# Query tiles 1 to 3 prepared inside the attention slots, with a new order of loads, wide weight loads and three result transfers

## What is computed

```python
def _qdq(x):
    s = jnp.maximum(jnp.max(jnp.abs(x), axis=-1, keepdims=True) / 127.0, 1e-08)
    return jnp.clip(jnp.round(x / s), -127.0, 127.0) * s

# x: (8, 56, 256), ctx: (8, 1500, 256), 16 heads of 16
q = _qdq(_layernorm(x)) @ _qdq(wq).T + bq
k, v = jnp.split(ctx @ wkv.T + bkv, 2, axis=-1)
attn = jax.nn.softmax(jnp.einsum('bnhd,bmhd->bhnm', q, k) * scale, axis=-1)
o = jnp.einsum('bhnm,bmhd->bnhd', attn, v).reshape(B, N, C)
x = x + jnp.tanh(g_xattn[0]) * (_qdq(o) @ _qdq(wp).T + bp)
x = x + jnp.tanh(g_ffn[0]) * experts(_layernorm(x))
```

## Time and profile before

| what | us |
|---|---|
| time, median of 3 runs (lowest, highest) | 400.9 (397.43, 401.9) |
| time of the profiled execution | 397.17 |
| its span, first to last instruction | 395.4 |
| first matmul | 11.33 |
| first scores, slot 0 | 32.71 |
| scores of slot 5 | 60.30 |
| scores of slot 56 | 272.69 |

### The profile page before, as it was taken

How to read it: one execution, slowest core, us unless ns; L and a number is a source line. 1 busy time by engine, 2 the same in 40 slices (tenths; PEclk the granted TensorE clock), 3 DMA queues, 4 the chain that set the end, 5 groups by cost and what they waited for, 6 DMA issues and landing times.

```text
span 395.4 us, 14055 instructions
## 1 busy us (share of the span) xinstructions
PE 351.7 (89%) x5828; PEld 262.6 (66%) x5828; DVE 302.6 (77%) x652; ACT 251.1 (63%) x413; POOL 105.8 (27%) x99
## 2 busy tenths in 40 slices
PE   0896859999998998999899999899986779999994
PEld 0672538677766865867686686677664557888883
DVE  3988885776676677568568667676988998999994
ACT  3575737687676776767667676657672355667671
POOL 6152643023132322302233230001010104544541
PEclk9999989999999999999999999999999999999998
DMA  7979995284187256329417313664200008654101
GB/s 250 208 173 194 214 186 115 67 173 122 54 143 196 58 91 160 99 82 159 147 56 117 91 33 70 126 156 149 76 3 3 0 2 282 181 159 125 51 2 46
DMA packets 34561, 45.67 MB, mean 115 GB/s; under 512 B 4043, under 2 KB 30347, under 8 KB 34371
## 3 DMA queue, kind: packets, MB, share of 16 engines
q1 hardware_dynamic: 33443, 43.74, 47.0%
q0 software_dynamic: 640, 0.78, 1.1%
q10 hardware_dynamic: 416, 0.26, 0.3%
HBM read 25.08 MB, written 0.47 MB: 65 GB/s over the span
## 4 chain that ended last, share of the span: by engine, by line
PE 76%; DVE 14%; issue 5%; ACT 2%; POOL 2%; DMA 1%; DVEq 0%; ACTq 0%; POOLq 0%
PE PS L1055 38%; PE PS L1121 10%; PE PS L1098 9%; PE PS L1132 8%; PE PS L1404 3%; PE PS L1363 3%; PE PS L1108 2%; DVE mx L809 2%; DVE mtop L813 2%; PE PS L1387 1%; DMA x_in<-x 1%; DVE st L712 1%; DVE KN L758 1%; DVE cT L730 1%; POOL cT L399 1%
## 5 line engine op out<-in xcount | busy, mean ns | idle before, releaser
L809 DVE TENSOR_REDUCE mx<-PS 112x1 f32<-112x500 f32 (+1 forms) x128 | 114.2, 933 | 53.9 <-PE PS L1098 53.8
L1055 PE MATMUL PS<-cT,wkvT 128*128 128x500 f16 x288 | 71.1, 384 | 21.9 <-POOL slot_of L408 11.3
L507 ACT ACTIVATE PT_all<-PS 128x1344 f32<-128x1344 f32 x64 | 82.5, 1289 | 12.3 <-PE PS L1121 9.6
L1055 PE MATMUL PS<-wkvT,cT 128*125 128x256 f16 x576 | 71.9, 275 | 0.0
L1055 PEld LDWEIGHTS PS<-wkvT,cT 128*125 128x125 f16 x576 | 63.9, 137 | 5.3 <-issue 0.5
L1055 PEld LDWEIGHTS PS<-cT,wkvT 128*128 128x128 f16 x288 | 27.4, 99 | 54.0 <-POOL rank L407 11.3
L399 POOL TENSOR_TENSOR cT<-c_in,cT 128x1000 f16<-128x1000 f32 x18 | 37.4, 2082 | 90.5 <-ACT cT L485 90.5
L492 ACT ACTIVATE KN<-PS,col_in 128x500 f16<-128x500 f32 x48 | 32.5, 677 | 41.1 <-PE PS L1055 41.1
L1098 PE MATMUL PS<-arena,QC 96*112 96x500 f16 x192 | 51.7, 376 | 3.5 <-issue 3.3
L1121 PE MATMUL PS<-QC,arena 98*128 98x112 f16 x768 | 48.6, 213 | 3.0 <-ACT QC L527 2.9
L499 ACT ACTIVATE V<-PS 125x512 f32<-125x512 f32 x48 | 28.7, 598 | 30.0 <-PE PS L1055 30.0
(11 more groups left out here) (211 smaller groups left out, 435.2 us busy)
## 6 DMA issues: line engine op xcount, KB each, us to landing
arena<-KN SPq DMA_DIRECT2D x144, 125.0 KB, 3.6
c_in<-ctx SPq DMA_DIRECT2D x24, 500.0 KB, 5.0
cT<-W SPq DMA_DIRECT2D x11, 352.0 KB
c_in<-W SPq DMA_DIRECT2D x6, 352.0 KB
cT<-W SPq DMA_DIRECT2D x11, 176.0 KB
arena<-place_far SPq DMA_DIRECT2D x1, 1568.0 KB, 10.2
c_in<-W SPq DMA_DIRECT2D x6, 176.0 KB
PT_all<-L_xattn_wkv SPq DMA_DIRECT2D x1, 512.0 KB, 6.1
```

The lines of the kernel that those rows point to most:

```text
L507: act.activation(PT_all[:, u % 4, :].rearrange("p (c k) -> p c k", c=CH), PS[:, 3:6, 0:4 * TP], ACT.Exp, scale=SCORE).then_inc(s["exp_done ...
L809: dve.tensor_reduce(mx[:, u % 2, k:k + 1], PS[0:TP, k:1 + k * (CH - 1), 0:CW], AX.XY, ALU.max).then_inc(s["red_done"], 1)
L1055: ins = mm(out_, w(a, h), x_(b, h), start=first and k == 0, stop=last and k == len(todo) - 1)
```

## The change

The edits, with the names of the diff:

- **Late tiles.** Only token tile 0 is prepared ahead of the slots. Tile t = 1, 2, 3 is prepared in slots 16(t-1)+1 to 16(t-1)+10, one step in each: `tile_step` on DVE (normalise, maximum, scale, round, spread), `tile_to_turn` and `tile_product` on PE in bank 7, `tile_turned`, `tile_scaled`, `tile_high` on ACT. The low half of a tile is written by DVE at the end of slot 16(t-1)+10. `qn` is a buffer of its own.
- **Stacking.** SP issues the 6 transfers of a tile (`stack_queries`), behind the stacking of the first half of the keys of batch 2t. `queries` of batch n waits for both tiles' halves by `q_stacked0` and `q_stacked1`. POOL issues none. The wait of the exponential is gone.
- **Loads.** The key half of the weights and chunk 0 of the context come first, then the tokens, the value half, the query weights, chunks 1 and 2. The rows and the gate weights move from ACT's queue to SP's. Chunk 2 of batch 1 is asked for behind the stacking of K2 and the queries. DVE begins with the weights and chunk 0, and takes the query weights before tile 0.
- **Blocks.** K5 of batch 0 moves into slot 0 as its first fill; in slots 0 and 1 of the first batch the fills are K0 and then K1 with K2.
- **Wide loads.** The weights of the values have 128 columns instead of 125, those of the scores 128 instead of 112.
- **Bias.** `biased_tokens` (the former L438 and L440) moves behind the queries of batch 5 on POOL.
- **Results.** Tiles 0 and 1 leave in one transfer, tile 2 in one, and tile 3 in one on ACT's queue.

```diff
+START = ("K0",), ("K1", "K2"), ("K3", "V0"), ("K4",), ("K5", "V1"), ("V2",), ("V3", "V4"), ("V5",)
...
+    fills = [(name[0], b + 1, int(name[1])) for name in (START if b == 0 else order)[i]] if b + 1 < B else []
+    if u == 0:
+        fills = [("K", 0, 5)] + fills
...
+def late_tile(u):
+
+    return u // (2 * NPAIR) + 1, u % (2 * NPAIR)
...
+            sp.dma_start(wkv_in[:, :, 0:D], wkv[:, :, 0:D]).then_inc(s["wk_loaded"], 16)
+            sp.dma_start(c_in[:, :, 0:CW], ctx_v[0, :, :, 0:CW]).then_inc(ctx_in[0], 16)
             sp.dma_start(x_in[:], x.rearrange("b s d -> (b s) d").rearrange("(t p) d -> p t d", p=TP)).then_inc(s["x_loaded"], 16)
-
-            sp.dma_start(wkv_in, wkv).then_inc(s["wkv_loaded"], 16)
-            for c in range(CH):
+            sp.dma_start(wkv_in[:, :, D:2 * D], wkv[:, :, D:2 * D]).then_inc(s["wv_loaded"], 16)
+            for k in range(NH):
+                sp.dma_start(wq_in[:, k, :], permuted(wq[k * 128:(k + 1) * 128, :])).then_inc(s["wq_loaded"], 16)
+            for c in range(1, CH):
                 sp.dma_start(c_in[:, :, c * CW:(c + 1) * CW], ctx_v[0, :, :, c * CW:(c + 1) * CW]).then_inc(ctx_in[c], 16)
...
+            def stack_queries(t):
+
+                for oh in range(NH):
+                    for k in (0, 1, 2):
+                        sp.wait_ge(s["qn_ready"], 2 * t + 1 + k // 2)
+                        sp.dma_start(q16[PW * k:PW * k + PW, 4 * oh:4 * oh + 4, t * TP:(t + 1) * TP], qn[:, oh, k // 2, :]).then_inc(s[f"q_stacked{oh}"], 16)
+
             load_context(1, 0)
+            sp.dma_start(row_in[:], rows.partition_broadcast(TP), allow_slow_non_contiguous=True).then_inc(s["rows_loaded"], 16)
+            sp.dma_start(gateT[:], gate).then_inc(s["rows_loaded"], 16)
             load_context(1, 1)
             stack_keys(0, 0, 0)
+            stack_keys(0, 0, 1)
+            stack_queries(0)
+            stack_keys(0, 0, 2)
             load_context(1, 2)
-            stack_keys(0, 0, 1)
-            stack_keys(0, 0, 2)
             for c in range(CH):
...
                 for c in range(CH):
                     stack_keys(b + 1, 0, c)
+                if b % 2 == 1:
+                    stack_queries(b // 2 + 1)
...
+            sp.wait_ge(s["y_final"], 2)
+            sp.dma_start(out_v[:, 0:2, :], y_out[:, 0:2, :]).then_inc(s["stored"], 16)
+            sp.wait_ge(s["y_final"], 3)
+            sp.dma_start(out_v[:, 2, :], y_out[:, 2, :]).then_inc(s["stored"], 16)
...
             def queries(n, k):
 
                 need(gp, "t_ready", NPAIR * (n - 2) + 4 * k + 4)
-                if n == 2:
-                    gp.wait_ge(s["q_rest"], 2 * 16 * 3)
+                gp.wait_ge(s[f"q_stacked{k}"], 16 * 3 * (n // 2 + 1))
...
+            queries(0, 0)
+            queries(0, 1)
+            gp.dma_start(KS[QR:QR + 2, 1], KS[QR:QR + 2, 0, 0:1, :].to_broadcast([2, NPAIR, KW])).then_inc(s["ones_spread1"], 16)
             for b in range(B - 1):
                 queries(b + 1, 0)
                 queries(b + 1, 1)
+                if b == 4:
+                    biased_tokens()
...
+            def tile_turned(t):
+
+                part = slice(t * TP, (t + 1) * TP)
+                act.wait_ge(s["late_turned"], t)
+                act.activation(xqT[:, :, part], bank16(7)[:, 0:NH * TP].rearrange("p (h t) -> p h t", h=NH), ACT.Copy).then_inc(s["late_copied"], 1)
+                act.activation(sx_row[:, part], PS[:, 7, 2 * TP:3 * TP], ACT.Copy).then_inc(s["late_copied"], 1)
+
+            def tile_scaled(t):
+
+                act.wait_ge(s["late_product"], t)
+                for oh in range(NH):
+                    act.activation(qT[:, oh, t * TP:(t + 1) * TP], PS[:, 7, oh * TP:(oh + 1) * TP], ACT.Copy,
+                                   scale=swq[:, oh:oh + 1]).then_inc(s["late_scaled"], 1)
+
+            def tile_high(t):
+
+                part = slice(t * TP, (t + 1) * TP)
+                act.wait_ge(s["late_rowed"], t)
+                for oh in range(NH):
+                    act.wait_ge(s[f"q_stacked{oh}"], 16 * 3 * t)
+                    act.activation(qT[:, oh, part], qT[:, oh, part], ACT.Identity, bias=bq_c[:, oh:oh + 1]).then_inc(s["qb_done"], 1)
+                act.wait_ge(s["qb_done"], NH * t)
+                act.activation(qn[:, :, 0, :], qT[:, :, part], ACT.Copy).then_inc(s["qn_ready"], 1)
...
+                if t < TT and step == 6:
+                    tile_turned(t)
+                elif t < TT and step == 8:
+                    tile_scaled(t)
+                elif t < TT and step == 9:
+                    tile_high(t)
...
+            def tile_step(t, step):
+
+                part = slice(t * TP, (t + 1) * TP)
+                d.settle()
+                if step == 1:
+                    d.did(normalise(x_in, xn, [t], 1))
+                elif step == 2:
+                    d.did(dve.tensor_reduce(am[0:TP, t:t + 1], xn[:, t, :], AX.X, ALU.max, apply_absolute_value=True))
+                elif step == 3:
+                    d.did(dve.tensor_scalar(sx[:, t:t + 1], am[0:TP, t:t + 1], 1.0 / 127, 1e-8, ALU.mult, ALU.max))
+                    d.settle()
+                    d.did(dve.reciprocal(am[0:TP, t:t + 1], sx[:, t:t + 1]))
+                elif step == 4:
+                    d.did(dve.tensor_scalar(xn[:, t, :], xn[:, t, :], am[0:TP, t:t + 1], 127.0, ALU.mult, ALU.min))
+                    d.settle()
+                    d.did(dve.tensor_scalar(xn[:, t, :], xn[:, t, :], -127.0, MAGIC, ALU.max, ALU.add))
+                elif step == 5:
+                    dve.tensor_scalar(xq16[:, t, :], xn[:, t, :], MAGIC, None, ALU.subtract).then_inc(s["xq_ready"], 1)
+                    spread_scales([t])
+                elif step == 8:
+                    dve.wait_ge(s["late_scaled"], NH * t)
+                    dve.wait_ge(s["late_copied"], 2 * t)
+                    dve.tensor_tensor(qT[:, :, part], qT[:, :, part], sx_row[:, part].unsqueeze(1).to_broadcast([128, NH, TP]),
+                                      ALU.mult).then_inc(s["late_rowed"], 1)
+                elif step == 10:
+                    dve.wait_ge(s["qn_ready"], 2 * t + 1)
+                    dve.tensor_tensor(qn[:, :, 1, :], qT[:, :, part], qn[:, :, 0, :], ALU.subtract).then_inc(s["qn_ready"], 1)
...
+                over = n > 0 and v % 2 == 1 and v < 5
+                need_lo(pe, n, v // 2 + over)
                 for k in range(2):
                     t = 2 * v + k
-                    last = split3(PS[0:KP, bank, k * D:(k + 1) * D], lambda a, h: cT[:, n % 2, a, h, t * KP:(t + 1) * KP],
+                    w = KP if n == 0 and t in (3, 7) else 128
+                    last = split3(PS[0:w, bank, k * D:(k + 1) * D], lambda a, h: cT[:, n % 2, a, h, t * KP:t * KP + w],
...
-                if i % 4 == 0:
-                    need(pe, "qc_done", 2 * b + i // 4 + 1)
+                if i in (0, 3):
+                    need(pe, "qc_done", 2 * b + (i + 1) // 4 + 1)
...
-                    mm(PS[0:TP, c, 0:CW], QC[0:QR, b % 2, i * TP:(i + 1) * TP], KS[0:QR, b % 2, i, c * CW:(c + 1) * CW],
+                    mm(PS[:, c, 0:CW], QC[0:QR, b % 2, i * TP:i * TP + 128], KS[0:QR, b % 2, i, c * CW:(c + 1) * CW],
...
+            def tile_to_turn(t):
+
+                take(("X", t - 1, 1))
+                pe.wait_ge(s["xq_ready"], t + 1)
+                turn_tokens(t, bank16(7))
+                pe.wait_ge(s["sx_diag"], t + 1)
+                spread(t, PS[:, 7, 2 * TP:3 * TP]).then_inc(s["late_turned"], 1)
+
+            def tile_product(t):
+
+                take(("Q", t - 1, 1))
+                pe.wait_ge(s["late_copied"], 2 * t)
+                project_queries(t).then_inc(s["late_product"], 1)
```

236 lines of the change are left out of this document (102 added, 134 removed).

## The result

The changed kernel is slower: 411.73 us median (410.6 to 414.69, 4 runs) beside 401.4 (397.43 to 402.78, 4 runs); ratio 1.030, 95% interval 1.025 to 1.036. I had forecast 400.0, range 393 to 405.5. The profiled execution took 410.6 us with a span of 408.8; the one of before, 397.17 and 395.4.

What follows compares the result with a forecast made beforehand. PE was taken as the bound, busy 351.7 of 395.4 us. Terms: 397.17 - 6.2 + 2.0 + 4.5 + 0.5 - 1.5 - 0.1 = 396.4 us profiled, so 400.0 median, range 393 to 405.5.

Steps and rivals of the forecast that it cites:

- The new wait on POOL: Slots 12, 28, 44: queries and two low halves in an unbroken POOL row delay `mtop`; cost 4.5 us, bounds 0 to 12.
- the long wait removed: Slot 3: `mtop`'s 5.62 us under POOL's row, PE's 4.31 us wait and the half clock behind it would go.
- The bias: Slot 32 on POOL: in a row with `mtop` of slot 33, waiting 1.7 us against 1.2 of cover; cost 0.5 us.
- The start: Up to slot 5: first scores over at about 30, slot 5 at 54.1 instead of 60.30; gain 6.2 us, bounds 3 to 10.
- They stand behind the low halves: Late tiles' ten DVE steps, 0.3 to 0.65 us each, would be ready before the next slot's scores need them.
- The late tiles: Tiles 1 to 3, moved into slots where PE is the bound: 0.65 us of PE work each; cost 2.0 us.
- The wide loads: Value and score weights of 128 columns: slightly shorter gaps at blocks and scores; gain 1.5 us, between 0 and 3.
- The results' 0.1: End of the kernel: the last tile's transfer starts 0.1 us earlier on its own queue; gain 0.1 us.
- The last stage: Behind slot 56: nothing was to change but the last transfers.
- The rows on POOL cost much: Rival: `mtop` waits 5 us at each of three rows, 12 us instead of 4.5; median 407.6 us, slower than before; chance 0.12.
- The rows cost nothing: Rival: DVE gets its turn between POOL instructions, or transfers land at another moment; 4.5 us less, median 395.6; chance 0.22.
- the same share (0.9%): Last step: the median lies 0.9% above the profiled execution, as before, turning 396.4 into 400.1, stated as 400.0 us.

Runs made afterwards that it cites:

- e1_order: Changed kernel with only POOL's order altered, two low halves going ahead of the queries of batches 2, 4 and 6: 401.78 us, ratio 0.999 to the kernel before.
- f3_narrow: Changed kernel with e1_order's POOL order, the bias moved to slot 56, and narrow weight loads (125 and 112 columns): 399.08 us, ratio 0.996 to the kernel before.

## Why the prediction was wrong

**The new wait on POOL** ("cost 4.5", 1.5 for each tile) is the term that failed, by size. The mechanism came as written, place by place. `mtop` waited 3.80, 4.22 and 3.48 us (3.4 forecast), PE 2.27, 2.46 and 1.95 (1.6, "up to 2.3"). But the slots grew by 4.0, 2.6 and 3.7 us against e1_order, 10.3 in all, 12 being the bound that I had given. The one without a fall of the clock cost just its wait; the other two cost 1.7 us more than theirs. I had written that fall into the long wait removed and not into the three added: a wait of PE of 2 us has a second price, which the earlier trace rows showed.

**The bias** ("cost 0.5", a wait of 1.7 us against a cover of 1.2) cost 4.0 us (slot 34, 8.07 against 4.05). The step that failed is that one operation waits once. Two were held in turn, 1.42 and 1.87 us, PE waited 2.37, and then ran at 0.50.

**The start** ("gain 6.2") gained 2.6, below the bound of 3. The chain on SP and ACT was right in kind: first scores over at 31.1 (30 forecast), chunk 0 of batch 2 landed at 41.9 (40.3), PE idle before slot 2's value block. The value block of slot 2 started at 46.1 and not at 42.9, and from there on the slots are 3.6 to 4.3 us late (49.4, 53.6 and 57.7 for 45.1, 49.8 and 54.1). Of these 3.2 us, 1.6 are the transfer. The other 1.6 are a step that I left out: behind the low half of K2 (43.70) DVE has in its order the tile's own first step (0.92) and then the reduction of slot 2's scores (1.77), and PE turns the maxima only behind the first part of that, at 46.00. "They stand behind the low halves" was true of the late tiles' steps, but here the reduction stood behind the step. The block itself took 0.9 us more by the clock. That the long wait of slot 3 goes was right.

**The late tiles** ("cost 2.0") cost about 2.2: the slot with the spread takes 4.47 for 4.14, the two behind it 4.20 and 4.13 for 4.01 and 3.92, so 0.7 a tile. **The wide loads** ("gain 1.5") gave some 0.8, by the slots that f3_narrow shows. The results' 0.1 can't be seen.

With 2.2 + 10.3 + 4.0 - 0.8 the stretch from slot 5 to slot 56 should be 15.7 us longer and is 13.0. The rest stands in PE's idle time there. All but the rows' and the bias's is the stops at fixed places of the program: before there are six, 6.4 us in all, and in the changed kernel three, 4.0 us in all. So 2.4 us were given back by a term that the prediction did not have: luck, without which the kernel would be slower still.

The last stage, put at nothing but the results' 0.1, took 3.0 us more by its clock. Together: 2.6 less, 13.0 and 3.0 more make the 13.4 us between the two profiled executions. Of the 14.2 us between the 396.4 forecast for the profiled execution and its 410.6, the rows are 5.8, the start 3.6, the bias 3.5 and the last stage 3.0; the late tiles and wide loads add 0.9, and the fixed stops take 2.4 off.

**The rivals.** "The rows on POOL cost much" came (407.6, chance 0.12), with a fourth place, and the clock in place of a later start of `mtop`. Its two figures hold slips: 12 in place of 4.5 makes 403.9 and not 404.6, and what decides against the change is 1.8 us a tile (the other gains of 5.3 by three), not 3.3. "The rows cost nothing" was refuted for rows without a pause, and its condition, that DVE gets its turn between two instructions, holds where POOL has to wait. To carry the profiled sum over to the median by the same share (0.9%) did not hold for the changed kernel, whose median lies 0.3% above its profiled execution: in the last stage the clock hardly fell in the profiled execution of before (0.99), and did fall in the other (0.94).

## What to carry to other kernels

In POOL's order look for instructions that can become ready together, since that row, not each instruction, is what DVE's smallest operations with two SBUF operands wait for; a wait ahead of one of them (a moved semaphore, work put behind a transfer) makes such rows. Price a wait of a busy PE by its length and the clock behind it, and price it with and without. When a stretch gets denser, look at the DMA share of it too: the next thing late may be PE's own instructions.

## What the runs showed of the hardware that I had not expected

- POOL's hold on DVE's operations with two SBUF operands outlasts its instruction while the next is ready, and ends at a wait for its own semaphore: 3.80 against 1.75 us for the same row.
- Behind PE's waits of 1.95 to 2.5 us the granted clock was 0.50 to 0.64 in most cases and 1.00 in one (after 164.2), and behind the same 2.35 us wait it differed between two kernels that are alike up to there. A wait of that length makes the low clock likely, not certain.
- PE stops at fixed places of its program, 618 or 619 matmuls apart, and goes on 1.2 to 1.9 us behind a 16 KB packet on the instruction queue. The stop is 4.26 and 6.18 us where the DMA queues are about full, and at the same place there is none where they are 39% busy.
